# When SyncE issues key factors, and where the next row is normalised, in an adjacency attention kernel

## The reference, cut to what matters

```python
q = relu(layernorm(x)) @ Wq.T + bq          # x: 4096 x 512
k = key @ Wk.T + bk                          # 4096 x 512
v = value @ Wv.T + bv
scores = einsum('nd,md->nm', q, k) / 64
s = scores * adj                             # adj: 4096 x 4096, 0 or 1
s = where(abs(s) < 1e-05, -1e9, s)
out = x + (softmax(s) @ v) @ Wm.T + bm
```

## Time and profile before

| | |
|---|---|
| median of 3 runs | 1559.7 us (1559.36 to 1562.26) |
| profiled execution | 1557.63 us |
| its span, first to last instruction | 1555.8 us |
| busy: TensorE, VectorE, ScalarE, GpSimd | 1517.8, 1137.9, 649.0, 219.3 us |
| moved by the SyncE queue | 300.50 MB |

### The profile page before, as it was taken

One profiled execution on the slowest core, in us unless ns is written; L12 is line 12 of the kernel. 1 busy time (PEld: TensorE's weight loads), 2 busy tenths in 40 slices (PEclk: granted clock), 3 DMA queues, 4 the chain that ended last, 5 costly groups with the idle time before them and its releaser, 6 DMA issues.

```text
span 1555.8 us, 23756 instructions
## 1 busy us (share of the span) xinstructions
PE 1517.8 (98%) x7010; PEld 692.4 (45%) x7010; DVE 1137.9 (73%) x2283; ACT 649.0 (42%) x1076; POOL 219.3 (14%) x285
## 2 busy tenths in 40 slices
PE   8998999999999999999999999999999999999998
PEld 5543444444444444444444444444444444444444
DVE  5989877777777677676767768676776867677672
ACT  5776444434343434344342434434343443434342
POOL 5164000000020102001020200202010020201000
PEclk9999999999999999999999999999999999999999
DMA  9834777667987878898787888878787887778855
GB/s 345 276 79 98 185 200 193 146 142 144 236 203 200 235 187 204 206 203 217 175 204 190 205 207 204 220 173 202 196 210 212 198 221 176 203 195 202 209 136 108
DMA packets 468579, 301.24 MB, mean 194 GB/s; under 512 B 378147, under 2 KB 390691, under 8 KB 468390
## 3 DMA queue, kind: packets, MB, share of 16 engines
q1 hardware_dynamic: 468512, 300.50, 76.5%
q10 hardware_dynamic: 6, 0.01, 0.0%
HBM read 189.54 MB, written 19.40 MB: 134 GB/s over the span
## 4 chain that ended last, share of the span: by engine, by line
PE 78%; DMA 8%; DVE 6%; issue 3%; ACT 3%; SPq 2%; DVEq 0%; ACTq 0%
PE R L874 12%; PE R L876 12%; PE R L875 12%; PE S L874 9%; PE S L876 9%; PE S L875 9%; DMA Kbuf<-key_factors 5%; PE M L874 3%; PE M L876 3%; PE M L875 3%; SPq L611 1%; DMA pT<-osb 1%; DVE Zbuf L1767 1%; PE R L992 1%; DMA pT<-ph 1%
## 5 line engine op out<-in xcount | busy, mean ns | idle before, releaser
L1369 ACT ACTIVATE drop<-Zbuf 128x512 f32<-128x512 f32 x256 | 161.0, 629 | 558.4 <-DVE cmx L1708 302.4
L874 PE MATMUL R<-Vbuf,pT 128*128 128x512 f16 x1008 | 382.1, 379 | 5.8 <-DMA pT<-ph 3.2
L876 PE MATMUL R<-Vbuf,pT 128*128 128x512 f16 x1008 | 382.0, 379 | 0.0
L875 PE MATMUL R<-Vbuf,pT 128*128 128x512 f16 x1008 | 382.0, 379 | 0.0
L874 PE MATMUL S<-Kbuf,qT 128*128 128x512 f16 x650 | 246.4, 379 | 4.3 <-DMA Kbuf<-key_factors 3.8
L875 PE MATMUL S<-Kbuf,qT 128*128 128x512 f16 x650 | 246.3, 379 | 0.0
L876 PE MATMUL S<-Kbuf,qT 128*128 128x512 f16 x650 | 246.3, 379 | 0.0
L1767 DVE SCALAR_TENSOR_TENSOR Zbuf<-S,rs,adjb 128x512 f32<-128x512 f32 x151 | 113.0, 748 | 90.8 <-PE S L876 80.7
L1821 DVE TENSOR_SCALAR drop<-drop,common 128x512 f32<-128x512 f32 x232 | 142.0, 612 | 50.0 <-ACT drop L1369 46.7
L1708 DVE CUSTOM_DVE_ANT_0 Zbuf<-drop,Zbuf 128x512 f32<-128x512 f32 x256 | 177.7, 694 | 0.0
L874 PEld LDWEIGHTS R<-Vbuf,pT 128*128 128x128 f16 x1008 | 98.6, 98 | 127.8 <-DMA pT<-ph 5.9
(11 more groups left out here) (277 smaller groups left out, 2005.2 us busy)
## 6 DMA issues: line engine op xcount, KB each, us to landing
Kbuf<-key_factors SPq DMA_DIRECT2D x161, 512.0 KB, 4.7
adjb<-in_adj_dram SPq DMA_DIRECT2D x256, 256.0 KB, 3.3
xq<-in_x_dram SPq DMA_DIRECT2D x32, 256.0 KB, 2.8
Kbuf<-in_L_gnn_key_dram SPq DMA_DIRECT2D x8, 1024.0 KB, 13.9
xr<-in_x_dram SPq DMA_DIRECT2D x32, 256.0 KB, 2.8
out_dram<-xr SPq DMA_DIRECT2D x31, 256.0 KB, 2.8
Vbuf<-in_L_gnn_value_dram SPq DMA_DIRECT2D x7, 1024.0 KB, 7.7
key_factors<-early SPq DMA_DIRECT2D x48, 128.0 KB, 2.3
```

The lines of the kernel that those rows point to most:

```text
L874: nc.tensor.matmul(ps, lhs[0], rhs[0], start=start, stop=False, skip_group_check=added)
L875: nc.tensor.matmul(ps, lhs[0], rhs[1], start=False, stop=False, skip_group_check=added)
L876: return nc.tensor.matmul(ps, lhs[1], rhs[0], start=False, stop=stop, skip_group_check=added)
L1369: nc.scalar.activation(drop[:, :], tile_of(s.i, s.j), ACT.Abs).then_inc(abs_ready, 1)
```

## The change

Two parts. In SyncE's queue the loads of `STARTS_*` for steps 3 to 6 (passes 4 to 15) move to the step before, ahead of its `load_probs`. The semaphore and the count are the same: `s.t + 1` one step earlier is `s.t`. What changes is what stands before them in the queue. The loads of steps 12 to 15 (`AHEAD`) stay. In step 5 of these passes `normalise` moves to VectorE's start of the step, the high half (`row_high`) ahead of ScalarE's absolute value, the low half (`row_low`) behind `tile_max` and ahead of the scores. Steps 14, and the passes before 4, stay as they are.

```diff
-            STARTS_TWO = {3: ((0, "T1"), 5), 4: ((1, "T1"), 4), 5: ((1, "T3"), 6), **AHEAD}
-            STARTS_THREE = {3: ((0, "T1"), 5), 4: ((2, "B11"), 4), 5: ((1, "T1"), 6), 6: ((2, "T1"), 5), **AHEAD}
+            AFTER_TWO = {2: ((0, "T1"), 5), 3: ((1, "T1"), 4), 4: ((1, "T3"), 6)}
+            AFTER_THREE = {2: ((0, "T1"), 5), 3: ((2, "B11"), 4), 4: ((1, "T1"), 6), 5: ((2, "T1"), 5)}
...
-                starts = STARTS_THREE if s.three else STARTS_TWO
-                if s.strassen and s.j in starts and (s.prefetch or s.j < 13):
-                    sp.wait_ge(kt_stored, 16 * (2 * len(PIECES) if s.three else 32))
+                if s.strassen and s.j in AHEAD and (s.prefetch or s.j < 13):
                     wait(sp, scores_done, s.t)
-                    load_factor(*starts[s.j])
+                    load_factor(*AHEAD[s.j])
...
                     turn_out(s, rows)
+                after = AFTER_THREE if s.three else AFTER_TWO
+                if s.strassen and s.j in after:
+                    what, q = after[s.j]
+                    sp.wait_ge(kt_stored, 16 * (2 * len(PIECES) if what[0] == 2 else 32))
+                    wait(sp, scores_done, s.t + 1)
+                    load_factor(what, q)
                 if s.early:
                     load_probs(s)
...
+                if s.early and s.halves_h is not None:
+                    row_high(s)
                 if s.early and s.c % 2 == 0:
                     weights_of(s)
...
                 if s.early:
+                    if s.halves_h is not None:
+                        normalise(s.halves_h)
                     probs_low(s)
                     tile_max(s)
+                    if s.halves_h is not None:
+                        row_low(s)
                     if s.c == 3 and s.has_out:
                         out_low(s)
...
-                if s.halves_h is not None:
+                if s.halves_h is not None and not s.early:
                     normalise(s.halves_h)
...
-                if s.halves_h is not None:
-                    wait(dve, h_hi, s.halves_h)
-                    wait(dve, rstd_ready, s.halves_h)
-                    nc.vector.scalar_tensor_tensor(out=row[:, 1, :], in0=xq[:, :], scalar=rstd[:, 2:3], in1=row[:, 0, :],
-                                                   op0=ALU.mult, op1=ALU.subtract).then_inc(h_split, 1)
+                if s.halves_h is not None and not s.early:
+                    row_low(s)
```

More of the change, by code:

```diff
@@ L1298, in high_of_mixes, with row_high @@
                     .then_inc(s_hi, 1)
+            def row_high(s):
+                wait(act, xn_ready, s.halves_h)
+                wait(act, rstd_ready, s.halves_h)
+                wait(act, q_in, 16 * (s.halves_h - 2))
+                wait(act, o_in, 16 * (s.halves_h - 4))
+                nc.scalar.activation(row[:, 0, :], xq[:, :], ACT.Copy, scale=rstd[:, 2:3]).then_inc(h_hi, 1)
             def weights_of(s):
@@ L1666, in query_low, with row_low @@
                 nc.vector.tensor_tensor(row[:, 1, :], xq[:, :], row[:, 0, :], ALU.subtract).then_inc(q_split, 1)
+            def row_low(s):
+                wait(dve, h_hi, s.halves_h)
+                wait(dve, rstd_ready, s.halves_h)
+                nc.vector.scalar_tensor_tensor(out=row[:, 1, :], in0=xq[:, :], scalar=rstd[:, 2:3], in1=row[:, 0, :],
+                                               op0=ALU.mult, op1=ALU.subtract).then_inc(h_split, 1)
             def out_low(s):
```

## The result

The changed kernel takes 1537.44 us in the median of four executions (1537.21 to 1538.11), the kernel before, beside it, 1559.53 us (1558.46 to 1562.26): ratio 0.9856, 95% interval 0.9839 to 0.9874, 22.1 us less. The forecast was 1541.2 with 1537.5 as the lower end of its range. The direction and the mechanism were right, the gain was 3.6 us larger than forecast, and the median lies just under the range.

What follows compares the result with a forecast made beforehand. TensorE, with work for 98% of the span, bounds the kernel; only its waits can be won. Factors 15.7 + second sum 3.5 = 19.2, less 0.7, is 18.5: 1559.7 - 18.5 = 1541.2 us, range 1537.5 to 1549.5 with two partial rivals.

Steps and rivals of the forecast that it cites:

- The factors: TensorE's waits for key factors in steps 4 to 6: loads issued 2.7 us earlier, all 15.7 us should go.
- What is pushed back: Transposes behind moved loads: issued at most 0.1 us later, landing 1.5 us later, at no cost.
- the cover: Spare 1.4 us between a transpose's landing and its use; without it, at most 1.5 us in each of four steps.
- Bandwidth: Transfers in steps 3 to 6: 6.55 MB in 23.3 us needs 281 GB/s, 81% of the best seen.
- soft point: Transfer room in steps 3 to 6: transposes dearer per byte, engine share already 0.96.
- this rival: Transfers become the bound and half of the 15.7 us stays: 1549.0 us, chance 0.11.
- The row: Next block's row work, moved ahead in step 5: L1744 0.95 us earlier, ending step 6's loss of 0.73 us.
- The margin in step 6: TensorE could start after L1744 at 1102.92 and wants to at 1103.15: 0.23 us to spare.
- The margin of step 4: TensorE could start after L1744 at 1090.05 + 0.13, 1090.18, and wants to at 1090.29: 0.11 us spare.
- allowance of 0.7 us for thin margins: Deducted from the gain for steps 4 and 6, 0.06 us per pass, a choice between 0 and 0.73.
- the sum: Total gain: 15.7 + 3.5 = 19.2 us, less 0.7, gives 18.5, subtracted from the median 1559.7: 1541.2 us.
- 19.2 us of waits: TensorE's listed waits, 430 to 1500 us, plus 0.16 each: factors 15.7, VectorE's second sum (L1744) 3.5.

Runs made afterwards that it cites:

- e1: The changed kernel with the next row's work back in its old place, only the factor loads moved: 1544.86 us, ratio 0.9912 to the kernel before.
- e11: The changed kernel with the load of (1,T1) alone back at the start of step 5: 1544.06 us, ratio 0.9905 to the kernel before.
- e5: The changed kernel with the factor load behind its step's transpose, still ahead of the adjacency load: 1539.45 us, ratio 0.9870 to the kernel before.
- e7: The changed kernel with an extra unread 512 KB DRAM copy ahead of the loads of steps 2, 3 and 4 of each pass: 1542.43 us, ratio 0.9890.
- e3: The kernel before, unchanged, profiled once more in one execution: 1560.34 us.
- e4: The kernel before, unchanged, profiled in a further single execution: 1556.97 us.
- e9: The changed kernel, unchanged, measured again: 1538.13 us, ratio 0.9866 to the kernel before.

## Why the prediction was right, and where it fell short

**The factors.** (0,T1) was to go 2.7 us earlier, behind nothing but the end of step 2's scores, and its stall of 1.21 us to vanish. It went 2.75 us earlier, the stall vanished, and so did all others; e1 has no factor wait at all. It landed 3.5 us after its issue, not at the 5.3 reckoned with, so the spare time was 3.5 us and not 1.5. That the head start did it is shown: e11 takes it back for one load, and the stalls return at that load's product alone; e5 gives 2.1 us of it back, and 1.3 us in two waits return.

**What is pushed back.** Transposes were issued no later and landed 0.4 to 2 us later, 1.1 in the mean, where 1.5 was forecast; the cover held. In the list between 430 and 1500 us the waits for transposed probabilities went from 1.3 us to 2.7, but the 1.3 us one lies at 1499.9 now, and lay at 1519.5, outside the list, before; without it they are 1.4 here too. Right.

**Bandwidth.** The "soft point" was not one. I had taken the share of 0.96 as nearness to a limit. e7 moved 332 GB/s at a share of 0.99, so there was more room than the chance of 0.11 for this rival reckoned with.

**The row.** The loss of 0.73 us in step 6 "whatever the factor does" was exact: e1 loses 0.72 us again in every pass of the loop. L1739's line was to start 2.7 us after step 6 starts; it starts at 1088.59 - 1086.39 = 2.20. The term that was off is GpSimd's root, whose middle step took 1.10 us in the pass of before that I had read, and 0.60 in this one; GpSimd, and what VectorE does beside it, before and after:

```profile
1096.46 1.10 POOL L720 TENSOR_TENSOR small<-small,fixed 128x1 f32<-128x1 f32 x1
...
1096.46 0.69 DVE L1698 SCALAR_TENSOR_TENSOR ph<-Zbuf,ph 128x512 f16<-128x512 f32 x1 [0.35 <-ACT ph L1341]
```

```profile
1084.23 0.60 POOL L724 TENSOR_TENSOR small<-small,fixed 128x1 f32<-128x1 f32 x1
...
1084.35 0.68 DVE L1713 SCALAR_TENSOR_TENSOR ph<-Zbuf,ph 128x512 f16<-128x512 f32 x1
```

This is no accident of one pass. Of the ten passes 5 to 14 the step took 1.10 us in five in the kernel before, in six and eight in e3 and e4, and in nine in e1, which leaves the row where it was. In each of these 28 VectorE's `probs_low` (L1698 in the kernel before) started within 3 ns of it; in the other twelve, where `probs_low` started 8 ns or more away, it took 0.55. In the changed kernel `normalise` stands ahead of `probs_low`, and the step took 0.60 in all ten. So moving the row also shortened the root by 0.5 us, which the prediction did not see. That the common start is the cause is read from this coincidence and was not tested by itself.

The margin in step 6 is 0.85 - 0.13 us in place of 0.23. The margin of step 4, put at 0.11, is as forecast (the same pass: the sum ends 4.30 us after the step starts, B22 starts at 4.54). So the allowance of 0.7 us for thin margins was not needed.

**The step that failed is the sum.** Measured gain 22.1, forecast 18.5. First, the 19.2 us of waits came from a list that leaves out short ones; the fine count has 21.3, of which 1.3 stay (two stalls of pass 4), so 20.0 went, 1.5 more than the 18.5. Of these 1.5 us, 0.8 are the short waits and 0.7 the allowance. The span fell by 19.5, half a microsecond less, since a few other waits grew. Second, and larger: I subtracted the waits of one execution, which took 1557.6 us, from a median of 1559.7, as if the 2.1 us between them were a fixed offset. They are not. e3 and e4 show that profiled executions of the kernel before differ by their waits for factors, and those go as well. That it is so in the executions without a profile too, on which the medians rest, is inferred. The profiled time less the waits, 1557.6 - 19.2 = 1538.4, or 1557.6 - 20.0 = 1537.6 by the fine count, would have been the better forecast for all executions; the changed kernel's two medians are 1537.4 and 1538.1. The median of 1559.5 was 1.9 us above its profile and that of the changed kernel 0.7 us below its own. 18.5 + 1.5 - 0.5 + 1.9 + 0.7 = 22.1. That the changed kernel's median lies under its profile is chance among executions 0.9 us apart; e9 has it 0.8 above. The lower end of the range had the same fault, and so lay 0.06 us above the median. On which side of that end a median of four falls is luck: e9, the same kernel again, gave 1538.13, inside the range. That the centre of the forecast was 3 to 4 us too high is not.

## What to carry to other kernels

Where the bound engine waits for something whose length varies from one execution to the next, a change that removes the wait removes that part of the scatter too: take the profiled time less the waits as the new level of all executions, and don't add back the distance to the median. In an in-order queue of transfers ask of each load not only which semaphore it waits for, but what is ahead of it that waits for a slower engine; and where two late things follow one another in the same step, price them together, since removing one alone may only uncover the other. Work that needs another engine's answer goes behind the request with other work between, so that the wait for it is short (0.37 us idle against 1.59), and ahead of a wait that is due anyway.

## What the runs showed of the hardware

The share of the transfer engines did not tell how full they were: the stretch of 24 us showed 1.04 at 271 GB/s in the changed kernel and 0.99 at 332 GB/s in e7. A transpose of 256 KB behind a factor of 512 KB in the same queue landed 0.4 to 2 us later than without it, 1.1 us in the mean of 44. The middle step of GpSimd's root (128x1) took 1.10 us in all 28 passes in which VectorE's `probs_low` started within 3 ns of it, and 0.55 in the other twelve of the same four executions.
